# Attention with half-row scores and a new order of each slot's steps

## The chip, the cores and the metric

One core of one Trainium2 chip runs the kernel. The metric is the device time of one execution in microseconds (us), here the median of three runs. Five engines work side by side and meet at semaphores: TensorE (PE, with its weight loads as PEld), VectorE (DVE), ScalarE (ACT), GpSimd (POOL) and SyncE (SP), which issues most DMAs.

## The reference

Four batches of 1024 rows and 256 columns pass an attention layer and a feed-forward layer with routed experts:

```
x = x + LN(attn_ref(LN(x)))      # attn_ref(z) = z + proj(softmax(q k^T / 4) v) + b, q, k, v from LN(z)*s+b
x = x + LN(ffn_ref(LN(x)))       # silu(x sw1) * (x sw2), LN, sw3; 512 rows also pass one of 8 experts
```

There are 16 heads of 16 columns. Every LN needs each row's mean and variance. All is f32 at the edges; q and k are split into three bf16 parts each, and six products of parts replace one f32 product.

## The kernel before

A unit `u` is one batch, one group of four heads and one half (512) of the queries; a batch has eight units. A unit takes eight *slots*, one per 128 keys, so a batch has 64. The slot number in a batch is `tau`, the batch `w`, and `t = 64 w + tau`. Slot `t` does the max products of slot `t` and, 12 slots behind (`e = t - LEAD`), the scores of slot `e`, and the value product of slot `e - 1`. Work of the layers around the attention is spread over the slots as *items*: `z`, `a`, `x`, `u` are four transposes each, `qk` and `v` projections of the next batch, `p`, `h`, `w` projections of the batch before, `mt` the transpose of a unit's row maxima, `ot` the four transposes of a unit's output.

The order of each engine's work is written out by hand in loops over `t`. On TensorE (L842 on for the helpers, L879 on for the slot) it is: scores, items, max products 0 and 1, value product, max products 2 and 3, `mt` or `ot`.

- *Max products* (L847): 128 queries by 512 keys, K = 48 rows. Heads with an even number lie on partitions 0 to 47, with an odd number on 64 to 111, so products 0 and 1 (and 2 and 3) take different halves of the array's rows and different banks. VectorE reduces each (L1083); at the unit's end L1086 negates the maxima, `mt` (L895) transposes them, L1091 and L1093 split them into two bf16 rows, and two DMAs of SP (L387, *mrow* here) put these in rows 48 and 49 of `qp`.
- *Scores* (L861): one product of K = 112 rows per head, with all six products of parts stacked (three on rows 0 to 47, three on 64 to 111) and 16 rows of ones and zeros between (`fixed`), which carry the negated maximum. ScalarE takes the exponential of two heads at a time (L687).
- *Value product* (L875): four heads at once on four 32-column tiles, f32.
- *The ring.* Max products and items share three PSUM banks in the order of `RING`. Whoever opens a bank waits until the step three places before it in that order has been taken out (`open_r`, L738). `RING_AT[t]` lists items first, then the four max products, then `mt` and `ot`. `s_free` guards the score banks likewise.
- *VectorE's side work* stands before the ring's work in a slot (L1163 to L1205): statistics for the LNs (`bn_stats` L1025, then the aggregation `bn_aggr` L1031), `residual` (L1073, the rest of q or k after its first bf16 part), gate products (L1060, L1062). GpSimd does the splits (L507, L510), the reciprocal roots, and scales the rows (`scaled` L466); its chains are called z, y, x, u and f after the LN that they serve, and `z_with_bias` (L485) prepares `x1`.
- ScalarE evacuates transposes and projections; for `qk` it copies the bank twice (L636 to `qkf`, L637 to `parts`). Twelve plus 24 DMAs per pair of projections (`pack_step`, L330) stack the parts into `kp` and `qp`.

The loop is followed by a tail with the last batch's feed-forward layer and the experts.

Of the kernel before, what the change touches and what calls it, by code (L numbers as in the profile page):

```python
# [6 lines left out]
P = 128  # L7
# [14 lines left out]
KM = 64 + KR  # L22
# [20 lines left out]
H_AT = (44, 45, 47, 48)  # L43


def ring_order():
# [3 lines left out]
    for t in range(SLOTS):  # L50
# [25 lines left out]
        row = fill  # L76
        if t < NS:
            row += [("max", t, j) for j in range(4)]
# [32 lines left out]
def max_column(t, j):  # L111
    h, qt, kh = max_item(t, j)
    return (h * QT + qt) * 2 + kh


def build(nc, x, ln_params, w_q, w_k, w_v, w_proj, b_proj, index_b, index_t, sw12, sb12, sw3, sb3,
# [10 lines left out]
    with ExitStack() as ctx:  # L127
# [47 lines left out]
        st6 = [sb(f"st6{i}", [P, NT, 6]) for i in range(2)]  # L175
        LN = ["z", "y", "x", "u", "f", "m", "g", "e", "o"]
# [36 lines left out]
        fixed = resid[0:16, :].bitcast(bf16)  # L213
# [112 lines left out]
        def _(sp):  # L326
# [3 lines left out]
            def pack_step(b, c, i):  # L330


                for n in range(3 * i, 3 * i + 3):
                    if n in (0, len(STACK)):
                        sp.wait_ge(s_third, 2 * KD * b + c + (n > 0) + 1)
                        if b > 0:
                            sp.wait_ge(s_av, SL * (b - 1) + (SL // 2 if c < 2 else SL))
                    par, row, k, q = STACK[n if n < len(STACK) else (n - len(STACK)) // NH]
                    rows, h0, src = slice(row, row + HD), c // 2 * 8 + par, slice(par * 64, par * 64 + 64)
                    if n < len(STACK):  # L340
                        sp.dma_start(kp[rows, h0:h0 + 7:2, :], parts[src, 0, k, :]).then_inc(s_pack[0], 16)
                    else:
                        qh = n % NH
                        sp.dma_start(qp[rows, qh, h0:h0 + 7:2, :],
                                     parts[src, 1, q, qh * HALF:(qh + 1) * HALF]).then_inc(s_pack[1], 16)
# [6 lines left out]
            sp.dma_start(kp[48:64, :, :], fixed[:, 0:N].rearrange("p (o n) -> p o n", o=1)  # L352
                         .to_broadcast([16, H, N])).then_inc(s_fixed, 16)
            sp.dma_start(qp[48:64, :, :, :].rearrange("p a h n -> p (a h) n"),
                         fixed[:, N:N + HALF].rearrange("p (o n) -> p o n", o=1)
                         .to_broadcast([16, NH * H, HALF])).then_inc(s_fixed, 16)
# [4 lines left out]
            for part in range(3):  # L361
                if part == 0:
                    sp.wait_ge(ra_free, TAKEN["qk", 0, 0, 1][1] + 1)
# [4 lines left out]
                for par, row, k, q in STACK:  # L368
                    if k == part:
                        sp.dma_start(kp[row:row + HD, par:par + 7:2, :], parts[par * 64:par * 64 + 64, 0, k, :])\  # L370
                          .then_inc(s_pack[0], 16)
            sp.wait_ge(s_third, 2)
            for par, row, k, q in STACK:
                sp.dma_start(qp[row:row + HD, 1, par:par + 7:2, :], parts[par * 64:par * 64 + 64, 1, q, HALF:N])\
                  .then_inc(s_pack[1], 16)
            sp.wait_ge(s_fixed, 32)
# [3 lines left out]
            for t in range(SLOTS):  # L380
                w, tau = divmod(t, SL)
                if t % 8 == 1 and 0 <= t // 8 - 1 < B * HU:
# [23 lines left out]
                if 2 <= w < B and tau == 4:  # L406
# [21 lines left out]
        def _(pool):  # L428
# [31 lines left out]

            def neg_of(k, a):
# [8 lines left out]
            def z_chain(b):  # L470
                a = b
                pool.wait_ge(s_xin, x_count("pre", b))
                rstd_of("z", b, 0, NT, a)
                neg_of("z", a)
# [22 lines left out]
            def residual(b, c):  # L497
                n = 2 * KD * b + c
                pool.wait_ge(ra_free, TAKEN["qk", b, c, 1][1] + 1)
# [29 lines left out]
            for t in range(SLOTS):  # L529
                w, tau = divmod(t, SL)  # L530
                if tau == 4 and w < B:
                    split(w, 2)
                if tau == 5 and w + 1 < B:
                    z_chain(w + 1)
                if tau == 6 and w < B:
                    residual(w, 3)
                    split(w, 3)
                if 1 <= w < B and tau == 15:
                    z_with_bias(w - 1)
                if 1 <= w < B and tau == 25:  # L540
                    rstd_of("y", w - 1, 0, NT, 0)
                    neg_of("y", 0)
# [6 lines left out]
                if 1 <= w < B and tau == 36:  # L549
                    rstd_of("x", w - 1, 0, NT, 0)  # L550
                    neg_of("x", 0)
# [4 lines left out]
                if 1 <= w < B and tau == 51:  # L556
                    rstd_of("u", w - 1, 0, NT, 0)
                    neg_of("u", 0)
                    pool.wait_ge(s_rstd["u"], w)
                    scaled(act, act, "u", 0, rstd["u"][:, 0, :], F).then_inc(s_norm["u"], 1)  # L560
                if 1 <= w < B and tau == 62:
                    rstd_of("f", w - 1, 0, NT, 0)
                    neg_of("f", 0)
                    pool.wait_ge(s_rstd["f"], w)
                    scaled(hid, hid, "f", 0, rstd["f"][:, 0, :], D).then_inc(s_norm["f"], 1)
                    pool.wait_ge(s_norm["f"], w)
                    nc.gpsimd.tensor_tensor(hid[:, :, :], hid[:, :, :], x1[:, :, :], ALU.add).then_inc(s_res, 1)

# [36 lines left out]
        def _(sc):  # L605
# [10 lines left out]
            def ring_item(key):  # L616
# [7 lines left out]
                elif kind == "qk":  # L624
# [11 lines left out]
                    nc.scalar.activation(qkf[:, half], src[:, :], ACT.Copy).then_inc(s_part, 1)  # L636
                    nc.scalar.activation(parts[:, c % 2, 0, half], src[:, :], ACT.Copy).then_inc(ra_free, 1)  # L637
# [28 lines left out]
            for part in range(3):  # L666
                if part == 0:
                    sc.wait_ge(ra_free, TAKEN["qk", 0, 1, 1][1] + 1)
# [4 lines left out]
                for par, row, k, q in STACK:  # L673
                    if q == part:
                        nc.scalar.dma_start(qp[row:row + HD, 0, par:par + 7:2, :],
                                            parts[par * 64:par * 64 + 64, 1, q, 0:HALF]).then_inc(s_q0, 16)
            sc.wait_ge(s_const, C_ALL)
            for t in range(SLOTS):
                w, tau = divmod(t, SL)
                e = t - LEAD  # L680
                items = [key for key in RING_AT[t] if key[0] in BY_ACT]
                for a in range(2):
# [6 lines left out]
                    for key in items:  # L689
                        if (key[0] in ("qk", "v")) == (a == 1):  # L690
                            ring_item(key)
# [45 lines left out]
        def _(pe):  # L737
# [90 lines left out]
            for t in range(SLOTS):  # L828
                e = t - LEAD

                def max_products(js):
# [11 lines left out]
                    for j in js:  # L843
                        h, qt, kh = max_item(t, j)
                        rows, h = slice(64 * (h % 2), 64 * (h % 2) + KR), g * GH + h
# [5 lines left out]
                def scores(a):  # L851
                    u, kt = e // 8, e % 8
                    g, qh = u % HU // NH, u % NH
                    dst = open_s(2 * e + a)
                    if e == 0 and a == 0:
                        pe.wait_ge(s_fixed, 32)
# [21 lines left out]

                if 0 <= e < NS:  # L879
                    scores(0)  # L880
                    scores(1)
                for key in RING_AT[t]:
                    if key[0] not in ("max", "mt", "ot"):
                        ring_item(key)
                if t < NS:
                    max_products(range(0, 2))
                if 0 <= e - 1 < NS:
                    value_product(e - 1)
                if t < NS:
                    max_products(range(2, 4))  # L890
# [5 lines left out]
                if e >= 0 and e % 8 == 2 and 0 <= e // 8 - 1 < B * HU:  # L896
# [5 lines left out]
                    ins.then_inc(r_full, 1)  # L902

# [114 lines left out]
        def _(ve):  # L1018
# [39 lines left out]
            def gate_product(n, a, h1, h2):  # L1058
                ve.wait_ge(s_he, n + 1)
                nc.vector.scalar_tensor_tensor(a, a, 1.0, h1, ALU.add, ALU.mult).then_inc(s_hc, 1)  # L1060
                ve.wait_ge(s_hc, 2 * n + 1)
# [343 lines left out]
```

## Time and profile before

| | |
|---|---|
| median of 3 runs | 1058.22 us (1057.33 to 1059.15) |
| profiled execution | 1057.63 us, of which the span of its trace is 1055.8 |
| mean granted TensorE clock | 0.972 |
| busy: TensorE, VectorE, ScalarE, GpSimd | 968.5, 866.2, 601.0, 253.8 us |
| chain of waits, by engine | TensorE 71%, VectorE 21%, DMA 2%, ScalarE 2% |
| chain, largest lines | scores L861 20%, value product L875 16%, reduction L1083 14%, max products L847 13% |

Busy time is the union of an engine's instructions. The ends of matmuls are modelled, so times between starts say more than durations. The first 45 us load and stack the first batch; slots without scores run to 84.8 us, the last value product ends near 935 us, and the tail takes the rest.

### The profile page before, as it was taken

What the parts mean: (1) busy time and instruction counts of PE and PEld (TensorE: products, weight loads), DVE (VectorE), ACT (ScalarE), POOL (GpSimd) and SP (SyncE); (2) the same over time, 40 slices, a digit from 0 to 9 for tenths busy, and PEclk for the clock granted to TensorE, in tenths of its full rate; (3) what the DMA queues carried; (4) which work ended last, traced back from release to release, by engine and by line L of the source; (5) the groups of instructions that cost most, each with busy time, mean ns of one, the idle gap of its engine ahead of it and who ended that gap; (6) DMA issues with size and microseconds to landing.
All of it is one profiled execution on the core that took longest, in us unless ns stands there. A gap on an engine that the chain in (4) does not pass through costs nothing.

```text
span 1055.8 us, 14476 instructions
## 1 busy us (share of the span) xinstructions
PE 968.5 (92%) x5346; PEld 382.8 (36%) x5348; DVE 866.2 (82%) x1759; ACT 601.0 (57%) x700; POOL 253.8 (24%) x309
## 2 busy tenths in 40 slices
PE   4279999999999999999999999999999999975985
PEld 2122322323334334333343344332432433234773
DVE  5287888999888988998879889989899899435766
ACT  3025677667775775767756765667656656741110
POOL 4060001100631231235404312053231010523022
PEclk9697999999999999999999999999999999997998
DMA  9905101330160113201611023012501000231001
GB/s 175 135 1 68 54 1 41 58 64 1 41 93 28 46 37 45 69 8 41 107 55 42 1 37 58 29 41 57 95 10 42 1 1 1 81 120 61 1 1 60
DMA packets 46534, 50.27 MB, mean 48 GB/s; under 512 B 8432, under 2 KB 39424, under 8 KB 46080
## 3 DMA queue, kind: packets, MB, share of 16 engines
q1 hardware_dynamic: 45120, 47.51, 21.4%
q10 hardware_dynamic: 960, 0.79, 0.7%
q0 software_dynamic: 384, 1.05, 0.3%
q8 instruction: 42, 0.69, 0.3%
q14 instruction: 28, 0.23, 0.1%
HBM read 13.94 MB, written 8.91 MB: 22 GB/s over the span
## 4 chain that ended last, share of the span: by engine, by line
PE 71%; DVE 21%; DMA 2%; ACT 2%; issue 2%; POOL 1%; SPq 1%; ACTq 0%; DVEq 0%; POOLq 0%
PE sc L861 20%; PE obank L875 16%; DVE mx L1083 14%; PE ring L847 13%; PE ring L762 9%; PE ring L784 4%; PE sc L950 3%; PE ring L754 2%; DVE st L1025 2%; PE ring L901 2%; ACT prob L687 1%; DVE hid L1047 1%; DMA kp<-parts 1%; DMA idx_in<-index_t 1%; PE ring L895 1%
## 5 line engine op out<-in xcount | busy, mean ns | idle before, releaser
L1083 DVE TENSOR_REDUCE mx<-ring 128x1 f32<-128x512 f32 x1024 | 649.9, 684 | 82.6 <-PE ring L847 74.9
L687 ACT ACTIVATE prob<-sc 128x1024 f32<-128x1024 f32 x512 | 501.0, 1022 | 269.7 <-PE sc L861 269.6
L875 PE MATMUL obank<-prob,vaug 128*32 128x512 f32 x2048 | 273.6, 606 | 0.7 <-ACT prob L687 0.7
L861 PE MATMUL sc<-qp,kp 112*128 112x512 bf16 x1024 | 268.4, 384 | 1.2 <-DMA qp<-mp 0.4
L847 PE MATMUL ring<-kp,qp 48*128 48x512 bf16 x1024 | 224.9, 391 | 32.6 <-issue 18.7
L847 PEld LDWEIGHTS ring<-kp,qp 48*128 48x128 bf16 x1024 | 57.5, 92 | 359.6 <-DVE mx L1083 188.8
L861 PEld LDWEIGHTS sc<-qp,kp 112*128 112x128 bf16 x1024 | 83.9, 98 | 115.5 <-issue 39.6
L507 POOL TENSOR_SCALAR parts<-resid 128x1024 bf16<-128x1024 f32 x14 | 14.7, 1050 | 328.9 <-DVE resid L1073 328.5
L875 PEld LDWEIGHTS obank<-prob,vaug 128*32 128x32 f32 x2048 | 40.3, 108 | 61.9 <-issue 52.4
L762 PE MATMUL ring<-w,yT 128*128 128x256 f32 x192 | 47.8, 389 | 1.4 <-ACT yT L613 1.4
L754 PE MATMUL ring<-ident,zn 128*128 128x128 f32 x128 | 21.1, 301 | 24.9 <-DVE zn L1041 12.8
L762 PEld LDWEIGHTS ring<-w,yT 128*128 128x128 f32 x192 | 37.2, 196 | 9.6 <-ACT yT L613 2.1
L1047 DVE TENSOR_TENSOR hid<-ring,b 128x512 f32<-128x512 f32 x32 | 21.9, 685 | 17.6 <-PE ring L762 17.5
L613 ACT ACTIVATE yT<-ring 128x512 f32<-128x512 f32 x32 | 18.6, 594 | 28.5 <-PE ring L754 28.5
L457 POOL TENSOR_SCALAR lv_y<-mv_y 128x8 f32<-128x8 f32 (+1 forms) x5 | 1.9, 373 | 133.8 <-DVE mv_y L1031 133.8
L762 PE MATMUL ring<-wv,zT 128*128 128x256 f32 x128 | 32.4, 398 | 1.6 <-DMA hln<-hidden_ln 1.3
L457 POOL TENSOR_SCALAR lv_u<-mv_u 128x8 f32<-128x8 f32 x4 | 1.1, 284 | 128.8 <-DVE mv_u L1031 128.8
L784 PE MATMUL ring<-zT,wk 128*128 128x512 f32 x64 | 30.5, 601 | 0.4 <-DVE mx L1083 0.2
L1103 DVE RECIPROCAL rsum<-ring 128x16 f32<-128x16 f32 x32 | 8.2, 258 | 27.2 <-PE ring L901 23.4
L784 PE MATMUL ring<-zT,wq 128*128 128x512 f32 x64 | 30.1, 595 | 0.2 <-DVE mx L1083 0.2
L510 POOL TENSOR_TENSOR parts<-resid,parts 128x1024 bf16<-128x1024 f32 x14 | 29.8, 2130 | 1.2
L762 PE MATMUL ring<-wp,yT 128*128 128x256 f32 x128 | 29.8, 379 | 0.0
(180 smaller groups left out, 787.8 us busy)
## 6 DMA issues: line engine op xcount, KB each, us to landing
kp<-parts SPq DMA_DIRECT2D x96, 128.0 KB, 5.3
qp<-parts SPq DMA_DIRECT2D x180, 64.0 KB, 2.6
x_sb<-x SPq DMA_DIRECT2D x7, 1024.0 KB, 5.9
out<-hid SPq DMA_DIRECT2D x4, 1024.0 KB, 4.6
x_scratch<-x SPq DMA_DIRECT2D x3, 1024.0 KB, 4.4
kp<-ew SPq DMA_DIRECT2D x1, 2048.0 KB, 8.4
x_sb<-x SPq DMA_DIRECT2D x2, 512.0 KB, 4.6
qp<-mp SPq DMA_DIRECT2D x64, 4.0 KB, 1.7
```

The lines of the kernel that those rows point to most:

```text
L510: nc.gpsimd.tensor_tensor(parts[:, c % 2, 2, :], resid[:, :], parts[:, c % 2, 1, :], ALU.subtract).then_inc(s_third, 1)
L687: nc.scalar.activation(prob[:, e % 2, 2 * a:2 * a + 2, :].rearrange("p g n -> p (g n)"), sbuf2[a][:, :], ACT.Exp, scale=0.25).then_inc(s_f ...
L754: ins = nc.tensor.transpose(dst[:, t * P:(t + 1) * P], src[:, 4 * h + t, kk * P:(kk + 1) * P], ident[:, :])
L762: ins = nc.tensor.matmul(dst[:, (t - 2 * i) * D:(t - 2 * i + 1) * D], src[:, k, t * P:(t + 1) * P], w[:, k, :], start=(k == 0), stop=(k == ...
L784: ins = nc.tensor.matmul(dst[:, :], w[:, k, mt * P:(mt + 1) * P], zT[:, k, h * HALF:(h + 1) * HALF], start=(k == 0), stop=(k == KD - 1))
L847: nc.tensor.matmul(dst[:, :], qp[rows, qh, h, qt * P:(qt + 1) * P], kp[rows, h, kh * HALF:(kh + 1) * HALF], start=True, stop=True).then_in ...
L861: ins = nc.tensor.matmul(dst[:, j * HALF:(j + 1) * HALF], kp[0:KM, h, kt * P:(kt + 1) * P], qp[0:KM, qh, h, :], start=True, stop=True)
L875: ins = nc.tensor.matmul(obank[i * VW:(i + 1) * VW, :], vaug[:, b % 2, kt, c0:c0 + VW], prob[:, v % 2, i, :], start=(kt == 0), stop=(kt == ...
L901: ins = nc.tensor.transpose(dst[:, c * P:(c + 1) * P], oT[:, u % 2, c * P:(c + 1) * P], ident[:, :])
L950: ins = nc.tensor.matmul(expert_bank(i)[:, t, :], lhs[:, m], w, start=False, stop=stop, skip_group_check=True)
L1047: return nc.vector.tensor_tensor(dst[:, t:t + 2, :], src[:, :].rearrange("p (t d) -> p t d", t=2), bias[:, :].rearrange("p (o d) -> p o d" ...
L1083: nc.vector.tensor_reduce(mx[:, u % 2, n:n + 1], src[:, :], AX.X, ALU.max).then_inc(rv_free, 1)
```

## The change

1. `STACK`, `plane_of`, `scores`: the six products of parts lie in two *planes* of `kp` and `qp`, each with three products on the 48 rows of the head's own half. Even heads stay on rows 0 to 47 and odd ones on 64 to 111 in both planes, and the second plane has two more rows for the maxima. A head's scores are two accumulating products, K = 48 and K = 50, and the two heads of a bank pair take the two halves of the rows. `fixed` is two rows of ones, copied by four small DMAs; the zero rows and the two large copies are gone.
2. The slot on TensorE: max products 0 and 1, scores, max products 2 and 3, items, `mt` or `ot`, value product. `RING_AT` lists the max products first.
3. mrow is four DMAs of half the size.
4. ScalarE does both exponentials first, then its items; the second copy of `qk` reads `qkf` instead of the bank.
5. The aggregation of the z, y, x, u and f statistics inside the loop goes from VectorE to GpSimd as eight small operations (`mean_of`), `residual(w, 2)` too. The tail and batch 0's z keep VectorE's.
6. VectorE reduces the slot's maxima before its side work. The gate product's halves are in slots of their own (47, 48, 50, 51), the u statistics in 50 and 51. The f statistics and chain move from slots 59 to 62 to slots 4 to 6 of the next batch (0 and 1 after the last), and the store of the result from slot 4 to slot 24.

```diff
-KM = 64 + KR
+KM = KR + 2
-STACK = [(par, (64 * (par ^ (r // 3)) + r % 3 * HD), k, q) for r, (k, q) in enumerate(PRODUCTS) for par in range(2)]
+STACK = [(par, r // 3 * 4, 64 * par + r % 3 * HD, k, q) for r, (k, q) in enumerate(PRODUCTS) for par in range(2)]
+F_AT = ((4, 5), (0, 1))
+GATE_AT = (47, 48, 50, 51)
...
-        row = fill
-        if t < NS:
-            row += [("max", t, j) for j in range(4)]
+        row = [("max", t, j) for j in range(4)] if t < NS else []
+        row += fill
...
+def plane_of(h, plane):
+    return h // 8 * 8 + 4 * plane + h % 8 // 2
...
-                    for j in range(2):
-                        sp.dma_start(qp[KR + j:KR + j + 1, qh, g * GH:(g + 1) * GH, :],
-                                     mp[:, u % 2, j, :]).then_inc(s_mrow[u % 2], 16)
+                    first = plane_of(g * GH, 1)
+                    for par in range(2):
+                        for j in range(2):
+                            row = 64 * par + KR + j
+                            sp.dma_start(qp[row:row + 1, qh, first:first + 2, :],
+                                         mp[GH // 2 * QT * par:GH // 2 * QT * (par + 1), u % 2, j, :])\
+                              .then_inc(s_mrow[u % 2], 16)
...
+            def mean_of(k, n, a, width):
+                half = st6[k == "z"]
+                mean0, sq0, mean1, sq1 = half[:, :, 1], half[:, :, 2], half[:, :, 4], half[:, :, 5]
+                pool.wait_ge(s_stats[k], n + 1)
+                nc.gpsimd.tensor_tensor(sum_m[:, :], mean0, mean1, ALU.add)
+                nc.gpsimd.tensor_tensor(dif_m[:, :], mean0, mean1, ALU.subtract)
+                step(nc.gpsimd.tensor_tensor(sum_q[:, :], sq0, sq1, ALU.add))
+                nc.gpsimd.tensor_scalar(neg[k][:, a, :], sum_m[:, :], -0.5, 0.0, ALU.mult, ALU.add)
+                nc.gpsimd.tensor_scalar(sum_q2[:, :], sum_q[:, :], 1.0 / width, 0.0, ALU.mult, ALU.add)
+                step(nc.gpsimd.tensor_tensor(dif_q[:, :], dif_m[:, :], dif_m[:, :], ALU.mult))
+                step(nc.gpsimd.tensor_scalar(dif_q2[:, :], dif_q[:, :], 0.25, 0.0, ALU.mult, ALU.add))
+                nc.gpsimd.tensor_tensor(mv[k][:, :, 1], sum_q2[:, :], dif_q2[:, :], ALU.add).then_inc(s_mean[k], 1)
...
-                    nc.scalar.activation(qkf[:, half], src[:, :], ACT.Copy).then_inc(s_part, 1)
-                    nc.scalar.activation(parts[:, c % 2, 0, half], src[:, :], ACT.Copy).then_inc(ra_free, 1)
+                    nc.scalar.activation(qkf[:, half], src[:, :], ACT.Copy).then_inc(ra_free, 1)
+                    sc.wait_ge(ra_free, TAKEN[key][1] + 1)
+                    nc.scalar.activation(parts[:, c % 2, 0, half], qkf[:, half], ACT.Copy).then_inc(s_part, 1)
...
-                        pe.wait_ge(s_mrow[u % 2], 32 * (u // 2 + 1))
-                    for j in range(2):
-                        h = g * GH + 2 * a + j
-                        ins = nc.tensor.matmul(dst[:, j * HALF:(j + 1) * HALF], kp[0:KM, h, kt * P:(kt + 1) * P],
-                                               qp[0:KM, qh, h, :], start=True, stop=True)
+                        pe.wait_ge(s_mrow[u % 2], 64 * (u // 2 + 1))
+                    for plane in range(2):
+                        h = plane_of(g * GH + 2 * a, plane)
+                        for j in range(2):
+                            rows = slice(64 * j, 64 * j + (KM if plane else KR))
+                            ins = nc.tensor.matmul(dst[:, j * HALF:(j + 1) * HALF], kp[rows, h, kt * P:(kt + 1) * P],
+                                                   qp[rows, qh, h, :], start=plane == 0, stop=plane == 1)
...
+                if t < NS:
+                    max_products(range(0, 2))
                 if 0 <= e < NS:
                     scores(0)
                     scores(1)
+                if t < NS:
+                    max_products(range(2, 4))
                 for key in RING_AT[t]:
                     if key[0] not in ("max", "mt", "ot"):
                         ring_item(key)
-                if t < NS:
-                    max_products(range(0, 2))
-                if 0 <= e - 1 < NS:
-                    value_product(e - 1)
-                if t < NS:
-                    max_products(range(2, 4))
...
+                if 0 <= e - 1 < NS:
+                    value_product(e - 1)
...
             for t in range(SLOTS):
                 w, tau = divmod(t, SL)
+                for key in RING_AT[t]:
+                    if key[0] == "max":
+                        ring_item(key)
...
                 for key in RING_AT[t]:
-                    if key[0] not in BY_ACT:
+                    if key[0] != "max" and key[0] not in BY_ACT:
                         ring_item(key)
```

## Rows read from the trace of the kernel before

**Rows 1.** The page, first part: busy us, share of the span and instructions of each engine.
```profile
PE 968.5 (92%) x5346; PEld 382.8 (36%) x5348; DVE 866.2 (82%) x1759; ACT 601.0 (57%) x700; POOL 253.8 (24%) x309
```

**Rows 2.** The timeline of TensorE over two slots: start us, us, engine, line, operation, out<-in, count.
```profile
496.04 1.03 PE L861 MATMUL sc<-qp,kp 112*128 112x512 bf16 x4
497.00 0.39 PE L847 MATMUL ring<-kp,qp 48*128 48x512 bf16 x2
497.32 1.06 PE L875 MATMUL obank<-prob,vaug 128*32 128x512 f32 x8
498.31 0.39 PE L847 MATMUL ring<-kp,qp 48*128 48x512 bf16 x2
498.64 1.04 PE L861 MATMUL sc<-qp,kp 112*128 112x512 bf16 x4
```

**Rows 3.** The same timeline, slots with a z item.
```profile
510.52 1.04 PE L861 MATMUL sc<-qp,kp 112*128 112x512 bf16 x4
511.40 0.60 PE L754 MATMUL ring<-ident,zn 128*128 128x128 f32 x4
511.93 0.43 PE L847 MATMUL ring<-kp,qp 48*128 48x512 bf16 x2
...
513.61 1.04 PE L861 MATMUL sc<-qp,kp 112*128 112x512 bf16 x4
```

**Rows 4.** The same timeline, starts of a v slot's scores and of the next.
```profile
426.44 1.04 PE L861 MATMUL sc<-qp,kp 112*128 112x512 bf16 x4
...
430.78 0.39 PE L861 MATMUL sc<-qp,kp 112*128 112x512 bf16 x1
```

**Rows 5.** The timeline before the scores begin: pair, item, pair; with what ended idle time.
```profile
69.12 0.39 PE L847 MATMUL ring<-kp,qp 48*128 48x512 bf16 x2
...
69.55 2.48 DVE L1083 TENSOR_REDUCE mx<-ring 128x1 f32<-128x512 f32 x4 [1.16 <-PE ring L847]
...
70.29 0.09 PEld L847 LDWEIGHTS ring<-kp,qp 48*128 48x128 bf16 x1 [0.32 <-DVE mx L1083]
...
70.89 1.59 PEld L762 LDWEIGHTS ring<-wv,zT 128*128 128x128 f32 x8 [0.51 <-DVE mx L1083]
...
72.82 0.39 PE L847 MATMUL ring<-kp,qp 48*128 48x512 bf16 x2
```

**Rows 6.** The windows view, from slot 15 to slot 256; us, then busy time of each engine.
```profile
97.05:907.49 810.44, 799.34 (x4604) 284.96 (x4603) 729.22 (x1396) 542.89 (x620) 182.20 (x219) 1.00 0.19 39
```

**Rows 7.** The timeline at the very first max products, weight loads and matmuls.
```profile
44.81 0.13 PEld L847 LDWEIGHTS ring<-kp,qp 48*128 48x128 bf16 x3 [19.05 <-issue]
44.84 1.00 PE L847 MATMUL ring<-kp,qp 48*128 48x512 bf16 x3 [18.68 <-issue]
```

**Rows 8.** The timeline around an mt transpose.
```profile
503.54 0.39 PE L847 MATMUL ring<-kp,qp 48*128 48x512 bf16 x2
...
503.99 0.28 PE L895 MATMUL ring<-ident,nm 128*16 128x128 f32 x1
...
504.10 1.03 PE L861 MATMUL sc<-qp,kp 112*128 112x512 bf16 x4
```

**Rows 9.** The timeline of VectorE: residual, x stats, second gate half, hidden stats.
```profile
189.28 1.22 DVE L1073 TENSOR_TENSOR resid<-qkf,parts 128x1024 f32<-128x1024 f32 x1
...
802.90 1.40 DVE L1025 BATCH_NORM_STATS2 st<-x 128x6 f32<-128x256 f32 x4
...
862.61 0.69 DVE L1062 SCALAR_TENSOR_TENSOR act<-act,hid 128x512 f32<-128x512 f32 x1
...
865.74 0.86 DVE L1025 BATCH_NORM_STATS2 st<-act 128x6 f32<-128x128 f32 x4
```

**Rows 10.** The timeline of GpSimd: a small operation and a residual.
```profile
493.05 0.20 POOL L477 TENSOR_TENSOR vn<-rr,mv_z 128x8 f32<-128x8 f32 x1
...
499.91 2.13 POOL L501 TENSOR_TENSOR resid<-qkf,parts 128x1024 f32<-128x1024 f32 x1
```

**Rows 11.** The timeline of SP: issue of the first two mrow DMAs.
```profile
81.25 1.22 SPq L387 DMA_DIRECT2D qp<-mp  x2
```

More of the change, by code:

```diff
@@ L212, in build @@
         mout = resid[:, 0:D]
-        fixed = resid[0:16, :].bitcast(bf16)
+        fixed = resid[0:2, 0:HALF].bitcast(bf16)
         sbuf2 = [ctx.enter_context(nc.psum_tensor(f"sc{i}", [P, 2 * HALF], f32)) for i in range(2)]
@@ L351, in _ @@
             sp.wait_ge(s_src, 1)
[L352 to L356, printed above, removed]
+            for par in range(2):
+                for h in (0, 8):
+                    first = plane_of(h, 1)
+                    sp.dma_start(kp[64 * par + KR:64 * par + KM, first:first + 4, :],
+                                 fixed[:, :].rearrange("p (o n) -> p o n", o=1).to_broadcast([2, 4, N]))                      .then_inc(s_fixed, 16)
             sp.dma_start(idx_in[:, 0, :], index_b.rearrange("(p c) -> p c", p=P)).then_inc(s_idxin, 16)
@@ L405, in _ @@
                     load_x(w + 2)
-                if 2 <= w < B and tau == 4:
+                if 2 <= w < B and tau == 24:
                     sp.wait_ge(s_res, w - 1)
@@ L531, in _ @@
                 if tau == 4 and w < B:
+                    residual(w, 2)
                     split(w, 2)
@@ L537, in _ @@
                     split(w, 3)
+                if 2 <= w <= B and tau == (6 if w < B else F_AT[1][1]):
+                    mean_of("f", w - 2, 0, D)
+                    rstd_of("f", w - 2, 0, NT, 0)
+                    pool.wait_ge(s_rstd["f"], w - 1)
+                    scaled(hid, hid, "f", 0, rstd["f"][:, 0, :], D).then_inc(s_norm["f"], 1)
+                    pool.wait_ge(s_norm["f"], w - 1)
+                    nc.gpsimd.tensor_tensor(hid[:, :, :], hid[:, :, :], x1[:, :, :], ALU.add).then_inc(s_res, 1)
                 if 1 <= w < B and tau == 15:
@@ L1112, in ring_item @@
                 elif kind == "h":
+                    if key[2] == 0 and key[1] > 0:
+                        ve.wait_ge(s_out, 16 * key[1])
                     add_bias(key, 2 * key[2], hid, b12)
@@ L1164, in _ @@
                 w, tau = divmod(t, SL)
+                for key in RING_AT[t]:
+                    if key[0] == "max":
+                        ring_item(key)
                 if tau in (2, 3) and w + 1 < B:
@@ L1171, in _ @@
                         ins.then_inc(s_stats["z"], 1)
-                if tau == 4 and w < B:
-                    residual(w, 2)
-                if tau == 5 and w + 1 < B:
-                    mean_of("z", w + 1, 0, NT)
+                if 2 <= w <= B and tau in F_AT[w == B]:
+                    i = F_AT[w == B].index(tau)
+                    for t2 in range(2):
+                        ve.wait_ge(rv_free, TAKEN["w", w - 2, 2 * i + t2][1] + 1)
+                    if i == 0:
+                        ve.wait_ge(s_mean["u"], w - 1)
+                    ins = stats_of("f", hid, 4 * i, 4, D)
+                    if i == 1:
+                        ins.then_inc(s_stats["f"], 1)
                 if 1 <= w < B and tau in (21, 22, 24, 25):
@@ L1178, in _ @@
                     ve.wait_ge(rv_free, TAKEN["p", w - 1, i][1] + 1)
+                    if i == 0 and w > 1:
+                        ve.wait_ge(s_mean["f"], w - 1)
                     ins = stats_of("y", x1, 2 * i, 2, D)
```

100 lines of the change are left out of this document (47 added, 53 removed).

## Prediction

> **What bounds the kernel now.** I read the page first. TensorE is busy for 92% of the span, VectorE for 82%, ScalarE for 57% and GpSimd for 24% [rows 1]; the chain of waits, read second, lies mostly on TensorE and for a fifth on VectorE (the table above has its shares). Busy TensorE is not yet a bound, since its ends are modelled, so I read the starts in the timeline next. A slot without side work lasts 2.61 us (496.04 to 498.64), made of scores 0.96 (496.04 to 497.00), max pair 0.32, value product 1.00 and max pair 0.32 [rows 2]. With one four-transpose item a slot lasts 3.08 us [rows 3], with a v item 4.34 [rows 4]. Each step follows the one before it with no wait. TensorE's order therefore sets the time. VectorE needs 0.60 us per reduction when they stand back to back ((2.48 - 0.68) / 3, the last counted to its end), so 2.39 us a slot: 0.22 below TensorE [rows 5].
>
> The steady part runs from slot 15's scores to those of slot 256: 241 slots in 810.44 us, all at full granted clock (1.00, the 2.4 GHz level), VectorE busy for 729.22 us of it [rows 6].
>
> **Where a slot pays today.** Four 512-column products stream for 0.86 us in the scores (x4 end 1.04 after the first start and one alone lasts 0.39, so (1.04 - 0.39) / 3 = 0.216 from start to start), yet the next step starts 0.96 after them. A max pair is concurrent (x2 in 0.39) and streams 0.21, yet 0.32 passes to the next step [rows 2]. So each change of tile shape costs about 0.11, and 0.14 behind the value product (1.00 against 0.86): 0.47 in a slot with four changes.
>
> **The change, part by part.**
>
> *Scores as two half-row passes.* Four K = 112 products become eight, in four pairs on rows 0 to 49 and 64 to 113, each pair in two banks. The max pair shows two such products going side by side [rows 2], so the four pairs take 4 x 0.216 = 0.86 us, as before. The second pass needs four more weight loads. Three loads of the max kind stood within 0.13 us, the third for the same rows as a product that had just begun [rows 7], so I cost them at nothing; if each of four pairs had to wait for its load, it is 4 x 0.09 (a load of this kind takes 0.09 [rows 5]) = 0.37 a slot, the upper bound.
>
> The Trainium skill (TensorE: Matmul & The Clock Gate, Part 3, The mechanism) says that a weight load overlaps a running matmul only where the row group differs. By that rule the second pass would pay for its loads, which is the last rival below; the three loads of rows 7 speak against it, and no run so far shows eight in a row.
>
> *The new order.* Max pair, scores, max pair are now one tile shape. A plain slot keeps two changes: 0.21 + 0.86 + 0.32 + 1.00 = 2.39 on TensorE alone, 0.22 less. In a slot with an item the saving is gone: pair to item, item to value product, value product to pair are three changes where four stood, and the first is larger, since pair to mt transpose takes 0.45 (503.54 to 503.99) where pair to value product takes 0.32 [rows 2, 8].
>
> The Trainium skill (TensorEngine Tiling, Tiling Modes, Key Properties) says that changing the tiling mode drains the engine. The 0.11 to 0.14 above agree; counting by this rule alone would give the faster rival below.
>
> *What the ring makes of it.* This step decides. The ring has three banks, so each step reuses the bank of the one three places before. In the new order the fourth max product needs the bank of the first, and the item behind it the bank of the second, in the same slot. The trace has that very sequence before the scores begin: pair at 69.12, first reduction at 69.55, the first bank's reuse at 70.29, the item (a v) at 70.89, the next pair at 72.82 [rows 5]. So from a pair's start the fourth product waits until 1.17 (TensorE would be there at 1.07), the item until 1.77 (without the wait 1.17 + 0.45 = 1.62 at the latest, and its weights would be in), and a v item that starts so takes 1.93. Before, the value product (1.00) stood between the pairs and scores between pair and item, and the waits were covered. With VectorE on time:
> - plain: 1.17 + 0.32 + 1.00 = 2.49 (now 2.61), 84 slots: 209.2
> - v, qk, p, h: 1.77 + 1.93 + 1.00 = 4.70 (now 4.33 for v), 60 slots, six with mt (+0.11 each) and three with ot (+0.43): 284.0
> - four transposes (z, a, x, u): 1.77 + 0.53 + 0.10 for the late weights + 1.00 = 3.40 (now 3.08), 41 slots, seven with mt: 140.2; ot alone, 27 slots, also four transposes: 91.8
> - w, half of v's products: 1.77 + 1.07 + 1.00 = 3.84, 12 slots: 46.1
> - mt alone: 1.77 + 0.11 + 0.11 + 1.00 = 2.99, 17 slots: 50.8
>
> Sum 822.1 us for the 241 slots. The item lengths are 0.53 [rows 3], 0.11 for mt [rows 8] and 1.93 [rows 5]; the 0.10 is 1.93 less eight starts of 0.216 and a change of 0.11. Each contains one change of shape behind the item. Item to value product is not in the trace; its bounds are 0 and 0.14 (the largest change), I take the 0.11 of item to pair, as the same tile is left. Over 157 slots the ends are -17 and +5 us.
>
> *VectorE's side work.* A plain slot of 2.49 leaves VectorE 0.10. What is put into a slot without a large item comes out on TensorE beyond that: nm (0.2 each, 24 times) 2.9; the first batch's residual at slot 44 (1.22 [rows 9]) 1.0; batch 3's x stats, twice 1.40 with 1.33 occupied [rows 9], 2.5; its gate halves with stats, twice 0.69 + 0.86 [rows 9], 2.8; its p slots about 1.5. Together 10.7 us, all of which the 810.44 already has in its own form. Nothing else is late: in a 4.70 slot VectorE has 2.3 us to spare. The five aggregations per batch that leave VectorE save it work but nothing on TensorE; f moves to item slots, where it is covered. If the cover were gone, each aggregation group would be worth under 0.7, as the f one.
>
> *GpSimd, ScalarE, SP.* GpSimd takes over residual(w, 2), 2.13 us, and eight operations of 0.20 per chain [rows 10], which I estimate at 2.2 us with their waits on each other. In batch 2, the fullest, residual, split, z chain, residual, split, f chain and z-with-bias add to about 45 us from slot 4, and the p item needs the last at slot 20, about 55 us on; nothing is behind it, zn is due at slot 10 (21 us on, done by 17). In the tail the f chain starts at slot 257 instead of 254 and z-with-bias ends some 28 us after slot 256, where x1 is first added 34 us after. ScalarE's second copy waits for the first: +0.2 per qk item, but its ring bank is free 0.5 sooner. mrow becomes four DMAs of SP instead of two: two more at about 0.57 (1.22 for two, the second issue's own time with it [rows 11]); behind them are queued the pack steps, 36 DMAs spread over 12 slots, due eight slots later. Only before slot 12 does TensorE wait for it: +1.1 us. The small fixed-row copies free DMA time before 19 us, where the stack waits for ScalarE's parts: 0 (bounds -2 and 0). Slot 0's v item, which runs today while TensorE waits for the stack, now stands behind the first pairs: +1.9 [rows 5].
>
> **Sum.** 822.1 + 10.7 - 810.4 + 1.1 + 1.9 = +25.4 us on the profiled execution's 1057.63, whose span is 1055.8: 1083.0. The median of the runs shown, 1058.22, is 0.6 above it: 1084. Here 0.2% (2 us) is about what a measurement can tell from no change.
>
> **The rivals.**
> *The waits do not bind (faster).* If TensorE's rhythm alone decided (the item's bank released within 1.3 us of the pair's start, where its weights would load), the slots are 2.39 plain, 3.06 with transposes, 4.33 with v, 2.75 with mt, 3.12 with ot, 3.48 with w: 763.5 + 10.7 against 810.4, +3.0 for start and mrow, so 1025. For it: 0.22 saved in 84 slots and the free VectorE. Against it: rows 5 show the wait whole. Chance 0.13.
> *No change.* If the item is held but item to value product costs nothing (-17) and VectorE's new places lose 8 us less than today's, it comes out near 1059. Chance 0.04.
> *Weight loads not hidden.* 0.37 x 256 = 95 us on top: 1178; decides as soon as a half-row product cannot have its successor's weights beside it. Against it rows 7. Should pairs not run side by side in the scores it is worse still. Chance 0.05.
> *Forecast,* 0.78, its own range 1066 to 1100.
>
> The range that leaves out 2 in 10: 1050 to 1102. Faster 0.14, same 0.04, slower 0.82.
>
> **What would show it.** Right: plain slots at 2.49, v slots at 4.70, z slots at 3.40 between scores' starts; weight loads of items and of the fourth max product ended by VectorE's reductions; the value product 0.32 behind the pair; four score pairs in 0.86. Wrong: items that start 0.45 behind the pair (first rival), score pairs over 0.22 apart (last), or a long wait for mrow, s_zb or GpSimd that I costed at nothing.

## The result, and the profile after

Before 1058.68 us, after 1078.63 (medians on one chip), ratio 1.0192, 95% interval [1.0173, 1.0212]: 1.9% slower. The profiled execution's span is 1076.1 us against 1055.8.

The page's first part and the window from slot 15's scores to slot 256's (columns as in [rows 1, 6]):

```profile
PE 958.6 (89%) x6372; PEld 388.5 (36%) x6372; DVE 843.0 (78%) x1634; ACT 605.0 (56%) x700; POOL 281.9 (26%) x418
```

```profile
98.08:926.71 828.63, 788.92 (x5568) 289.79 (x5564) 705.42 (x1272) 545.40 (x619) 201.47 (x306) 1.00 0.18 39
```

Matmuls and VectorE are less busy than before, at the same clock (1.00), and the same 241 slots take 18.2 us more: TensorE was without a matmul for 11.1 us of them before (810.44 - 799.34), now for 39.7. Of the other 2.1 us of the span, 1.0 lies ahead of slot 15 (97.05 to 98.08) and 1.1 behind slot 256 (149.4 against 148.3).

TensorE's timeline: an ot slot, a plain slot, and a z slot (answers to [rows 2, 3]):

```profile
503.41 0.39 PE L876 MATMUL ring<-kp,qp 48*128 48x512 bf16 x2
503.63 1.03 PE L894 MATMUL sc<-qp,kp 48*128 48x512 bf16 x8
504.51 0.46 PE L876 MATMUL ring<-kp,qp 48*128 48x512 bf16 x2
505.18 0.66 PE L932 MATMUL ring<-ident,oT 128*128 128x128 f32 x4 [0.21 <-DVE mx L1122]
505.76 1.06 PE L908 MATMUL obank<-prob,vaug 128*32 128x512 f32 x8
506.76 0.39 PE L876 MATMUL ring<-kp,qp 48*128 48x512 bf16 x2
506.99 1.03 PE L894 MATMUL sc<-qp,kp 48*128 48x512 bf16 x8
507.86 0.46 PE L876 MATMUL ring<-kp,qp 48*128 48x512 bf16 x2
508.25 1.06 PE L908 MATMUL obank<-prob,vaug 128*32 128x512 f32 x8
509.25 0.39 PE L876 MATMUL ring<-kp,qp 48*128 48x512 bf16 x2
...
515.05 1.03 PE L894 MATMUL sc<-qp,kp 48*128 48x512 bf16 x8
515.93 0.46 PE L876 MATMUL ring<-kp,qp 48*128 48x512 bf16 x2
516.69 0.63 PE L783 MATMUL ring<-ident,zn 128*128 128x128 f32 x4 [0.30 <-DVE mx L1122]
517.25 1.06 PE L908 MATMUL obank<-prob,vaug 128*32 128x512 f32 x8
518.24 0.39 PE L876 MATMUL ring<-kp,qp 48*128 48x512 bf16 x2
518.47 1.03 PE L894 MATMUL sc<-qp,kp 48*128 48x512 bf16 x8
```

The plain slot lasts 2.49 (506.76 to 509.25), the z slot 3.42 between scores' starts (3.08 before). The pair passes to scores after 0.22, scores to the pair after 0.87: the changes of tile shape are gone. But the pair behind the scores is stretched (0.46 for two products that take 0.39 side by side) and the item starts 0.67 behind it, released by VectorE. The weight loads show both:

```profile
506.77 0.75 PEld L894 LDWEIGHTS sc<-qp,kp 48*128 48x128 bf16 x8
507.64 0.10 PEld L876 LDWEIGHTS ring<-kp,qp 48*128 48x128 bf16 x1
507.93 0.09 PEld L876 LDWEIGHTS ring<-kp,qp 48*128 48x128 bf16 x1 [0.19 <-DVE mx L1122]
```

The eight loads of the scores take 0.75 beside the running products, so they cost nothing. The fourth product's load starts 1.17 after the slot's first pair (506.76 to 507.93), when VectorE has read the first bank.

Slots by kind, from start to start of the scores, counted over the 241 slots (mean us, from the starts in each trace; e1 to e9 are the experiments below):

```
kind              count  before  after  foreseen   e1    e2    e4    e9    e6
plain                84   2.70   2.58    2.49*    2.70  2.58  2.69  2.66  2.44
four transposes      34   3.17   3.39    3.40     3.16  3.11  3.17  3.14  3.03
ot                   27   3.39   3.35    3.40     3.16  3.39  3.25  3.25  2.99
mt                   17   3.00   2.97    2.99     2.81  3.17  2.96  3.27  2.62
qk, v                27   4.33   4.68    4.70     4.50  4.43  4.33  4.92  4.32
p, h                 24   4.48   4.72    4.70     4.64  4.51  4.47  4.53  4.33
w                    12   3.63   3.84    3.84     3.79  3.67  3.60  3.67  3.47
241 slots, us           810.4  828.6   832.8    815.9 810.2 804.4 833.3 759.1
```

\* the 10.7 us of VectorE's side work, which I had put on the plain slots, come on top. The remaining 16 slots hold two items.

### The profile page after: what moved, and what is told of

It reads as the page before. It is cut to its first block and busy times, and to the rows that moved or that the text cites. A ratio compares the mean times of both kernels' runs of the same rounds, so it can differ in the third digit from the quotient of the medians.

```text
span 1076.1 us, 16570 instructions
## 1 busy us (share of the span) xinstructions
PE 958.6 (89%) x6372; PEld 388.5 (36%) x6372; DVE 843.0 (78%) x1634; ACT 605.0 (56%) x700; POOL 281.9 (26%) x418
## 5 line engine op out<-in xcount | busy, mean ns | idle before, releaser
L1122 DVE TENSOR_REDUCE mx<-ring 128x1 f32<-128x512 f32 x1024 | 635.0, 682 | 130.2 <-PE ring L876 128.8
L894 PE MATMUL sc<-qp,kp 48*128 48x512 bf16 (+1 forms) x2048 | 268.4, 379 | 0.8 <-ACT prob L716 0.2
L876 PE MATMUL ring<-kp,qp 48*128 48x512 bf16 x1024 | 231.3, 389 | 32.3 <-DMA qp<-parts 22.5
L876 PEld LDWEIGHTS ring<-kp,qp 48*128 48x128 bf16 x1024 | 73.0, 93 | 334.2 <-DVE mx L1122 200.8
L894 PEld LDWEIGHTS sc<-qp,kp 48*128 48x128 bf16 (+1 forms) x2048 | 99.3, 95 | 103.8 <-ACT prob L716 15.7
L481 POOL TENSOR_TENSOR sum_m<-st 128x8 f32<-128x8 f32 x15 | 3.1, 209 | 272.6 <-DVE st L1058 272.6
L530 POOL TENSOR_TENSOR resid<-qkf,parts 128x1024 f32<-128x1024 f32 x8 | 17.1, 2133 | 216.3 <-ACT parts L667 216.3
L665 ACT ACTIVATE qkf<-ring 128x512 f32<-128x512 f32 x32 | 19.1, 596 | 36.8 <-PE ring L813 35.4
L675 ACT ACTIVATE vaug<-ring 128x512 f32<-128x512 f32 x16 | 9.6, 597 | 46.0 <-PE ring L791 46.0
```

The lines of the kernel that those rows point to most:

```text
L876: nc.tensor.matmul(dst[:, :], qp[rows, qh, h, qt * P:(qt + 1) * P], kp[rows, h, kh * HALF:(kh + 1) * HALF], start=True, stop=True).then_in ...
L894: ins = nc.tensor.matmul(dst[:, j * HALF:(j + 1) * HALF], kp[rows, h, kt * P:(kt + 1) * P], qp[rows, qh, h, :], start=plane == 0, stop=pla ...
L1122: nc.vector.tensor_reduce(mx[:, u % 2, n:n + 1], src[:, :], AX.X, ALU.max).then_inc(rv_free, 1)
```

## The experiments

Times are told as ratios to the kernel before on the same chip (after: 1.0192); one hundredth is 10.6 us.

**The order, the half rows and the side work, each alone (e1 to e4).**

```diff
 # e1: the value product goes ahead of items, mt and ot
                     max_products(range(2, 4))
+                if 0 <= e - 1 < NS:
+                    value_product(e - 1)
                 for key in RING_AT[t]:
 # e2: scores, items, pair, value product, pair; ring, VectorE, ScalarE as before; half rows stay
 # e3: the order of after; KM = 64 + KR, scores and stacking as before
 # e4: e2 and e3 together: only the side work and ScalarE's second copy stay changed
```

> The changed kernel with the value product moved ahead of the items (and of mt and ot): max pair, scores, max pair, value product, items. The ring's order is untouched. Theory (an item waits for the bank of the same slot's second max product, at 1.77 us from the pair's start): the value product fills the wait, an item starts at about 2.6 us without waiting, slots with four transposes fall from 3.39 to about 3.14, with v or qk from 4.68 to about 4.43, mt 2.97 to 2.8, plain stays 2.49 to 2.58; in all some 38 us less than 1078.6: 1040 (1030 to 1050), under the kernel before. Rival 1 (the item slots are dearer for their changes of tile shape and for f32 weights loaded late): three changes stay, 1073 to 1079. Rival 2 (VectorE's and GpSimd's moved work costs the 20 us): unchanged, 1075 to 1080.

Measured: 1066.83 us, 1.0102 [1.0077, 1.0127]. A miss by 27 us. The slots whose item ScalarE reads gained all or most of what I had expected (four transposes 3.39 to 3.16, qk and v 4.68 to 4.50, foreseen 3.14 and 4.43). What VectorE must read gained little or lost it again: p, h and w slots fell by 0.05 to 0.08, the ot slot fell from 3.35 to 3.16, and the plain slots, some of them behind an ot or mt, rose from 2.58 to 2.70. Timeline of TensorE in e1, an ot and the plain slot behind it:

```profile
501.70 0.66 PE L934 MATMUL ring<-ident,oT 128*128 128x128 f32 x4
502.29 0.39 PE L876 MATMUL ring<-kp,qp 48*128 48x512 bf16 x2
502.51 1.03 PE L894 MATMUL sc<-qp,kp 48*128 48x512 bf16 x8
503.38 0.76 PE L876 MATMUL ring<-kp,qp 48*128 48x512 bf16 x2
504.07 1.06 PE L908 MATMUL obank<-prob,vaug 128*32 128x512 f32 x8
```

And VectorE at that place:

```profile
502.39 0.26 DVE L1142 RECIPROCAL rsum<-ring 128x16 f32<-128x16 f32 x1 [0.27 <-PE ring L934]
502.68 0.42 DVE L1148 TENSOR_TENSOR anat<-ring,rsum 128x256 f32<-128x256 f32 x1
503.02 2.47 DVE L1122 TENSOR_REDUCE mx<-ring 128x1 f32<-128x512 f32 x4
```

The ot tile comes just ahead of the next pair, so the first reduction starts 0.73 behind the pair's start (502.29 to 503.02) instead of 0.42, and the fourth product of that slot stretches its pair to 0.76. The wait has moved one slot on.

> The changed kernel with the slot's order of the kernel before (scores, items, max pair, value product, max pair; ring, ScalarE and VectorE accordingly), half-row scores and the moved side work kept. Theory: the value product and the scores again lie between what shares a bank; max pair to scores has no change of shape, so a plain slot is about 2.5 (the second max product waits for the third's bank, 1.17 after it), transposes 3.15, v and qk 4.4: about 1040 (1030 to 1050). Rival (half-row scores are dear in themselves, eight weight loads or eight products): no better than 1058, up to 1080.

Measured: 1061.4 us, 1.0049 [1.003, 1.0067]. A miss by 21 us. Plain slots fell to 2.58 as in after, but each item now stands between two steps of half-row shape: scores to item is 0.96, against 0.87 behind full-row scores, and a v item's start to the pair 1.93 against 1.82 (medians of the starts in the two traces). A z slot of e2 (answers to [rows 3]):

```profile
509.11 1.03 PE L896 MATMUL sc<-qp,kp 48*128 48x512 bf16 x8
510.07 0.65 PE L785 MATMUL ring<-ident,zn 128*128 128x128 f32 x4
510.66 0.39 PE L878 MATMUL ring<-kp,qp 48*128 48x512 bf16 x2
```

The kinds that I had priced came out near it (2.58, 3.11 and 4.43, foreseen about 2.5, 3.15 and 4.4; some 6 us over the window). The slots that I had not priced are dearer too: from mt or ot to the next scores 0.21 and 0.59 pass here, 0.11 and 0.49 in e4, and the mt and ot slots take 3.17 and 3.39 (2.96 and 3.25 in e4). Over the 241 slots all this gives back what the plain slots win over before (810.2 against 810.4).

> The changed kernel with the scores of the kernel before (one product of K = 112 per head, its stack of rows, its two mrow DMAs, its large fixed-row copies), the new order and the moved side work kept. Theory: the item still waits until 1.77 us after the pair, so items as in the changed kernel (3.40, 4.70), while a plain slot has its four changes again (2.61): 1078.6 + 84 x 0.1 = about 1087 (1080 to 1094). Rival (the half-row scores cost the 20 us): 1055 to 1062.

Measured: 1088.45 us, 1.0298 [1.0278, 1.0317]. As expected.

> Old order and old scores with the moved VectorE and GpSimd work alone (f chain, gates, aggregation, residual), and ScalarE's second copy from qkf. Theory: the order of TensorE decides and this part is worth little: 1052 to 1060, gaining up to 5 us where slot 62 of three batches took 4.48 instead of 3.23. Rival (the moved side work costs the 20 us): 1070 to 1080.

Measured: 1052.76 us, 0.9967 [0.9947, 0.9986]. As expected, and faster than both kernels (than the one before by 0.3%). Its window is 804.4 us:

```profile
95.42:899.82 804.40, 796.93 (x4604) 284.47 (x4603) 715.34 (x1273) 546.27 (x620) 201.56 (x306) 1.00 0.19 40
```

Read together, by the ratios: with full rows the new order costs 35 us (e3 less e4), with half rows 15 (after less e2). The half rows win 11 us in the new order (e3 less after) and lose 9 in the old one (e2 less e4). The side work's new places win 3.5 us (1.5 to 5.6).

**Who reads the item (e5).**

```diff
+                    if key[0] in ("p", "h", "w"):   # read by VectorE: with mt, ot ahead of the value product
+                    if key[0] not in ("max", "mt", "ot", "p", "h", "w"):   # read by ScalarE: behind it
```

> The changed kernel, with the value product moved ahead of those items only that ScalarE evacuates (z, a, x, u, qk, v); the items that VectorE evacuates (p, h, w, mt, ot) stay ahead of the value product. Theory V (VectorE's order of work sets the time: what it must read besides the row maxima makes its next reductions late, so it doesn't matter on which side of the value product its items stand): within 4 us of e1_value_first, 1063 to 1071. Theory P (each place in the order has its own price on TensorE, and an item behind the first pair costs 0.1 to 0.3 more wherever it is read): 27 ot, 24 p and h, 17 mt and 12 w at 0.2 us dearer than in e1, 1080 to 1085.

Measured: 1065.43 us, 1.0074 [1.0057, 1.0091]. Theory V. For mt, ot, p, h and w together it makes hardly a difference on which side of the value product they stand: the mt and ot slots are back at 2.97 and 3.35, p and h at 4.72, and the plain ones fell from 2.70 to 2.60.

**A shorter reduction (e6 to e8).**

```diff
-    nc.vector.tensor_reduce(mx[:, u % 2, n:n + 1], src[:, :], AX.X, ALU.max).then_inc(rv_free, 1)
+    nc.vector.tensor_reduce(mx[:, u % 2, n:n + 1], src[:, 0:HALF // 2], AX.X, ALU.max).then_inc(rv_free, 1)
```

> The changed kernel, with one thing different: VectorE takes each row's maximum over the first 256 of the 512 columns of its tile (the second half of each is left out), so its reduction is about 0.3 us shorter and nothing on TensorE changes. Theory V (the ring's buffers come free only when VectorE has read them, and in this order that ends last in most slots): the plain slot falls from 2.49 to about 2.39, the slot with four transposes from 3.39 to about 3.06, with qk or v from 4.68 to about 4.35, and the time to 1022 (1012 to 1035). Theory T (TensorE's own rhythm in the new order costs this): within 5 us of 1078.

Measured: 1002.67 us, 0.9487 [0.9464, 0.951]. Theory V, but 19 us faster than I gave it, outside its range. Its window, slot 15 to slot 256, and TensorE's timeline over an a slot:

```profile
91.69:850.79 759.10, 758.36 (x5566) 272.69 (x5563) 474.55 (x1273) 545.26 (x620) 201.60 (x306) 1.00 0.19 42
```

```profile
503.24 1.04 PE L894 MATMUL sc<-qp,kp 48*128 48x512 bf16 x8
504.12 0.38 PE L876 MATMUL ring<-kp,qp 48*128 48x512 bf16 x2
504.43 0.66 PE L783 MATMUL ring<-ident,anat 128*128 128x128 f32 x4
505.01 1.06 PE L908 MATMUL obank<-prob,vaug 128*32 128x512 f32 x8
506.01 0.39 PE L876 MATMUL ring<-kp,qp 48*128 48x512 bf16 x2
```

TensorE is without a matmul for 0.7 us of the window. The item starts 0.31 behind the pair, no stretch is left. 69.5 us of the gain lie in the window and 6.4 ahead of it, where no scores stand between the max products and they wait for reductions; I had priced neither this nor what delays the plain slots beyond 2.49.

> e1_value_first with each row's maximum taken over the first 256 of 512 columns, as in e6. Theory V: 1020 (1010 to 1032), near e6, since with a fast VectorE the order of the slot hardly matters. Theory T (its 27 us over the 1040 that I expected of e1 are TensorE's own): within 5 us of 1067.

Measured: 1019.58 us, 0.9634 [0.9618, 0.965]. The number is right, its reason is not: I had called it near e6, and it is 17 us slower. The order of after is the better one here too, but not by TensorE's own steps: where nothing waits these are the same in both traces (from the second pair to what follows 0.31, value product 1.00, four transposes 0.59). What e7 has more are waits. TensorE is without a matmul for 6.8 us of its window of 776.2, and from the second pair to the value product it takes 0.37 in the mean; the stretches stand in slots behind mt, ot, p, h, w and some qk, and none behind four transposes or v. I read this as items that VectorE or ScalarE takes out too late for the pairs right behind them, even when the reductions are short.

> e4_side_work_only (order and scores of the kernel before, only the side work as in the changed kernel) with each row's maximum taken over the first 256 of 512 columns. Here TensorE sets the rhythm of the plain slot (2.61), so a shorter reduction takes away only the stalls of slots with side work and of the pre-summed items: 1044 (1040 to 1049). Were VectorE the limit of this kernel too, as theory V says of e1 and e6, it would fall by 30 us or more, to 1022.

Measured: 1021.47 us, 0.9657 [0.9636, 0.9678]. A miss, on the side of the theory that I had not followed for this kernel: the old order too loses some 31 us to VectorE's reductions (29 between the profiled executions, 33 by the ratios). Its window, and an mt (the answer to [rows 8]):

```profile
89.92:870.24 780.32, 779.70 (x4604) 278.11 (x4602) 469.94 (x1272) 546.15 (x620) 200.90 (x306) 1.00 0.19 41
```

```profile
509.61 0.39 PE L874 MATMUL ring<-kp,qp 48*128 48x512 bf16 x2
509.93 0.28 PE L924 MATMUL ring<-ident,nm 128*16 128x128 f32 x1
510.05 1.03 PE L890 MATMUL sc<-qp,kp 112*128 112x512 bf16 x4
```

Pair to mt is 0.32 here. The 0.45 of [rows 8] was a wait for a bank, not the price of a change of shape. 24 us of these lie in the window, none of them in slots with qk or v alone.

e6 against e8 is what order and half rows are worth where TensorE hardly waits: windows of 759.1 and 780.3 us, 21 us less. Long reductions add 24.1 us to the window of the old order (e4 less e8) and 69.5 to that of the new one (after less e6), and that turns the sign.

**Another bank for the item (e9, e10).**

```diff
-        row = [("max", t, j) for j in range(4)] if t < NS else []
+        row = [("max", t, j) for j in range(2)] if t < NS else []
         row += fill                                 # then mt, ot
+        row += [("max", t, j) for j in range(2, 4)]
```

> The changed kernel with the slot in a third order: first pair of row maxima, scores, the items (with mt and ot), second pair, value product; the ring, VectorE and ScalarE follow it (ScalarE takes a transposed item between its two exponentials, qk and v behind both, as in the kernel before). The item now takes the ring's third buffer, which has been free since the slot before, and not that of the first pair's second product, so it needn't wait for VectorE's second reduction (that wait is 0.36 us of the 0.668 from the second pair to the item in the changed kernel, 0.310 in e6 where the reductions are short). Theory V: the slot with four transposes 3.39 to about 3.13, with qk or v 4.68 to 4.43, with p or h 4.72 to 4.45, with mt 2.97 to 2.73, with ot 3.35 to 3.1, with w 3.84 to 3.55, plain 2.49 as it is: 40 us over 241 slots, 1040 (1034 to 1052). Rival: VectorE reads mt, ot, p, h and w ahead of the second pair and its reductions then end after the next slot has begun, so the wait only moves (as in e1): 1062 to 1070.

Measured: 1084.46 us, 1.0258 [1.0235, 1.028]. A miss by 44 us, and worse than the rival. Slots with four transposes fell as foreseen, those with ot, p, h and w by four to seven tenths of it (the table), qk and v rose to 4.92, mt to 3.27. An ot slot of e9, TensorE and VectorE:

```profile
506.85 0.39 PE L879 MATMUL ring<-kp,qp 48*128 48x512 bf16 x2
...
507.16 1.40 DVE L1061 BATCH_NORM_STATS2 st<-hid 128x6 f32<-128x256 f32 x4
...
508.47 1.28 DVE L1125 TENSOR_REDUCE mx<-ring 128x1 f32<-128x512 f32 x2
509.20 0.09 PEld L879 LDWEIGHTS ring<-kp,qp 48*128 48x128 bf16 x1 [0.75 <-DVE mx L1125]
...
509.80 0.09 PEld L879 LDWEIGHTS ring<-kp,qp 48*128 48x128 bf16 x1 [0.51 <-DVE mx L1125]
```

The second pair now ends the slot's ring work, so the slot's side work (here 1.40 of statistics) is queued right ahead of the next slot's first reductions, which start 1.62 behind their pair, and products three and four wait. In the order of after the item gives VectorE that time. This is a reading of one place; I didn't test how much of the 44 us it is.

The rise of qk and v is another wait. VectorE's residual now stands behind the second pair, which itself stands behind the item of 1.92 us, and ScalarE's next copy into `qkf` waits for the residual (`s_resid`). VectorE, ScalarE and TensorE in the first of three such places:

```profile
165.36 1.22 DVE L1115 TENSOR_TENSOR resid<-qkf,parts 128x1024 f32<-128x1024 f32 x1
166.66 0.60 ACT L667 ACTIVATE qkf<-ring 128x512 f32<-128x512 f32 x1 [3.17 <-issue]
167.31 0.39 PE L879 MATMUL ring<-kp,qp 48*128 48x512 bf16 x2 [2.19 <-ACT qkf L667]
...
168.50 3.68 PE L816 MATMUL ring<-zT,wq 128*128 128x512 f32 x4
```

TensorE stands still for 2.2 us, and behind it the granted clock is 0.66 over 5 us (168 to 173), and the next item takes 3.61 to the pair instead of 1.92. In all the twelve slots with the second projection (`wq`) take 5.52 in the mean against 4.42 for the first (`wk`) where it stands alone: 13 us of the 44. With them at 4.42 the kind would be at the 4.43 that I foresaw. No run isolates this either.

> e9_items_between with the full-row scores of the kernel before. Scores of full rows cost 0.2 more in a plain slot (0.32 + 0.97 against 0.23 + 0.87) and about 0.08 less in a slot with an item (half-row scores to item 0.963 against 0.874, item to pair 0.10 more). Theory V: 84 plain slots by 0.15 (part of it the wait that binds anyway) less 133 item slots by 0.08, so within 8 us of e9: 1042 (1034 to 1056). If the first pair of reductions is what the slot waits for, the slower scores hide it and it is equal to e9 within 3 us.

Measured: 1078.13 us, 1.0181 [1.0152, 1.021]; e9 is slower by 0.0077, 8 us. The number fails with e9's; the difference is at the edge of what I allowed.

**Load or release (e11, e12).** A short reduction frees a bank sooner and also takes load off VectorE. These two take off the same load at different places.

```diff
-    src[:, :]
+    src[:, 0:HALF // (2 if j < 2 else 1)]     # e11; e12: j >= 2
```

> The changed kernel; of each slot's four reductions the two of the first pair (before the scores) take their maximum over the first 256 of 512 columns only, 0.34 us from start to start in place of 0.60; the second pair's are whole. VectorE has 0.52 us less to do in each slot, as in e12. Theory B (what costs is the buffer's release in the slot: the fourth product waits for the first reduction, the item for the second): both waits go, items 0.31 behind the pair in place of 0.67, and nearly all of e6's 76 us comes: 1008 (1002 to 1018). Theory L (what costs is VectorE's load as such: 2.39 us of reductions in a slot of 2.49): half of e6's gain, 1040 (1030 to 1050).

Measured: 1011.88 us, 0.9564 [0.9542, 0.9587]; window 766.0.

> The same, with the second pair's two reductions over 256 of 512 columns and the first pair's whole. The same load is taken off VectorE, but the two waits inside the slot stay (plain slots 2.49, four transposes 3.39, qk 4.68). Theory B: only what VectorE's side work delays is won, 84 plain slots by 0.09 (from a mean of 2.58 to 2.49) and some 2 us ahead of slot 15: 1068 (1060 to 1074). Theory L: as e11, 1040 (1030 to 1050).

Measured: 1071.01 us, 1.0125 [1.0105, 1.0145]; window 822.2. Theory B in both. One slot with four transposes of each, e12 first:

```profile
514.86 1.03 PE L894 MATMUL sc<-qp,kp 48*128 48x512 bf16 x8
515.73 0.46 PE L876 MATMUL ring<-kp,qp 48*128 48x512 bf16 x2
516.40 0.66 PE L783 MATMUL ring<-ident,zn 128*128 128x128 f32 x4 [0.21 <-DVE mx L1122]
```

```profile
508.23 1.04 PE L894 MATMUL sc<-qp,kp 48*128 48x512 bf16 x8
509.10 0.38 PE L876 MATMUL ring<-kp,qp 48*128 48x512 bf16 x2
509.41 0.66 PE L783 MATMUL ring<-ident,anat 128*128 128x128 f32 x4
```

The same 0.52 us a slot taken off VectorE is worth 7 us behind the second pair and 66 ahead of it: 0.0067 and 0.0628 of the time before. In the order of after it is the release of the first pair's banks inside the slot that costs, not VectorE's load.

## Why the prediction was right

- *TensorE's own cost* (2.39 plain, the loads of the half-row products hidden, pairs side by side): right. Eight loads take 0.75 beside the products, pair to scores 0.22, scores to pair 0.87. With short reductions (e6) the kinds are 2.44 (plain), 3.03 (four transposes), 4.32 (v), 2.99 (ot), 2.62 (mt) and together 759.1, against 2.39, 3.06, 4.33, 3.12 and 2.75 in my first rival. Its kinds add up to 761.5, not to the 763.5 that I wrote, so it should have said 1023. It was near what TensorE can do, in part by luck: I had 0.45 from pair to item, which is 0.31, and 1.81 from a v item to the value product, which is 1.92, and in its v slot the two errors nearly cancel.
- *The ring* (1.17 for the fourth product, 1.77 for the item): right, the step that decided. Fourth load at 1.17, item at 1.77 (503.41 to 505.18). The sequence before the scores begin [rows 5] was a true sample, and e11 and e12 show the cause alone.
- *The sums by kind*: the item kinds of the table are within 0.05 of what I gave. The 0.10 for late weights has the right size for a v item, but the wrong reason: in e6, where its weights wait for nothing, it takes the same 1.92. Four transposes take 0.59, not 0.63.
- *Side work*: mis-sized. I gave 10.7 us, the window holds 828.6 - 822.1 = 6.5 beyond the sum by kinds: 7.9 more in the plain slots and some 1.3 less in the others.
- *Start*: mis-sized. I gave +3.0 for the v item and mrow; the first scores start 1.9 later (84.80 to 86.69), slot 15 only 1.0. The tail's +1.1 I had not given. Together 20.3 of span against the 25.4 foreseen.
- *What bounds the kernel before*: half right. I wrote that each step follows the one before it with no wait, and read pair to mt's 0.45 as a price of shape. e8 shows waits of 0.13 in each mt and ot slot, and some 31 us in all went with the long reductions. It didn't change the sum, since in the new order the item's wait covers it, but it made the first rival dearer, and it misled me on the old order in e8.
- *The Trainium skill's rule on weight loads* (TensorE: Matmul & The Clock Gate, Part 3, The mechanism): this trace doesn't bear it out for these tiles. Successive pairs of the scores use the same two row groups, and their eight loads (0.75 us) are hidden all the same, with the pairs 0.22 apart. The same section also lets a load go ahead into the background weight buffer, which would fit; no run here tests it.

## What to carry to other kernels

Before you move a step, follow each buffer of the ring from writer to reader to next writer: a step that stood between two uses of a buffer was covering its release, even if it was put there for another reason. Shortening one of two equal loads of an engine at a time tells whether its load or its latency is what others wait for. And an engine that is busy 78% of the time can still be worth 7% of it.

## What the runs showed of the hardware

- A reduction of 128x512 from a ring bank follows another after 0.60 us, one of 128x256 after 0.34 (e6 has 0.42 as mean length of one, after 0.68).
- Scores pass to a step that takes the array's rows as they do after 0.87 (half rows to pair in after, full rows to a 128x128 f32 item in before) and to one that takes them otherwise after 0.96 to 0.97 (half rows to item in e2, full rows to pair in before), though both kinds of scores stream alike. That is one change of shape, about 0.10, and it goes by the two shapes that meet. From item to pair e2 needs another 0.05 (four transposes) to 0.10 (a v item) more than before; the runs don't show why.
- The granted clock was 1.00 in the windows of the kernels before and after, of e4, e6 and e8, whether TensorE idled for 39.7 us, in short waits, or 0.7. In e9, behind each of three waits of 2.2 us in one piece, it was 0.57 to 0.66 over the next 5 or 6 us, and 1.00 again in the 5 or 6 us after.
